# Delta by ScalarE's softplus, read from the side bank, in a macaron block of gated FFNs around a state-space layer

## The reference

```python
xn = x * rsqrt(mean(x * x) + EPS) * norm_w
skip = xn @ W_skip.T
u = silu(causal_conv4(xn @ W_in.T) + conv_b)
delta = softplus(u @ Wd1.T @ Wd2.T + bd2)            # 1024 x 512 for each batch
Bt, Ct, A = u @ WB.T, u @ WC.T, -exp(A_log)
h_l = exp(delta_l * A) * h_(l-1) + (delta_l * u_l) * B_l    # scan over 512 positions, 16 states
y_l = sum over states of h_l * C_l
out = ((y + u * W_D) * silu(skip)) @ W_out.T
```

## Time and profile before

| | |
|---|---|
| Median of 3 runs | 4050.57 us (4049.12 to 4053.82) |
| Profiled execution | 4051.71 us, its span 4050.0 us |
| Log blocks | 16, the first starting at 345.9 us, the last at 3558.7 us |
| Scan | the first Exp of a unit at 360.5 us, the last product with C starts at 3826.4 us |

### The profile page before, as it was taken

The page is one execution under the profiler, slowest core; times in us unless marked ns, Lnnn a source line. Parts: engine busy times, 40 slices in busy tenths (PEclk is TensorE's granted clock), DMA queues, the critical chain, the costliest instruction groups (busy, mean ns, idle before and its releaser), DMA issues. The chain is left out here.

```text
span 4050.0 us, 38161 instructions
## 1 busy us (share of the span) xinstructions
PE 3607.4 (89%) x11264; PEld 2077.2 (51%) x11264; DVE 3205.8 (79%) x3392; ACT 2039.0 (50%) x2694; POOL 2918.7 (72%) x2249
## 2 busy tenths in 40 slices
PE   7998889999999999899999898899887788787798
PEld 5654555555555555554555454545454344444455
DVE  4425988787989789887999889977988789989823
ACT  3234557547554664557554755466353665353310
POOL 0024789677977899688886998779967989878700
PEclk9999999999999999999999999999898898888899
DMA  6444545544645465354554555546454345444432
GB/s 234 148 134 140 162 147 168 201 148 148 211 159 182 146 202 191 120 187 154 201 172 154 173 164 188 155 139 202 156 171 133 124 148 180 148 126 148 122 123 90
DMA packets 233148, 647.64 MB, mean 160 GB/s; under 512 B 25968, under 2 KB 26224, under 8 KB 223216
## 3 DMA queue, kind: packets, MB, share of 16 engines
q1 hardware_dynamic: 159216, 510.95, 37.0%
q10 hardware_dynamic: 73728, 134.25, 12.5%
HBM read 579.57 MB, written 65.54 MB: 159 GB/s over the span
## 5 line engine op out<-in xcount | busy, mean ns | idle before, releaser
L1096 POOL TENSOR_TENSOR db<-du,Bb 128x512 f32<-128x512 f32 x1024 | 1357.5, 1326 | 539.8 <-DVE decay L990 459.9
L990 DVE TENSOR_TENSOR_SCAN decay<-decay,db 128x512 f32<-128x512 f32 x1024 | 1251.9, 1223 | 268.7 <-ACT decay L690 253.8
L1107 POOL TENSOR_TENSOR y<-y,pr 128x512 f32<-128x512 f32 x1024 | 1382.8, 1350 | 63.9 <-DVE pr L1000 63.9
L690 ACT ACTIVATE decay<-delta,aneg 128x512 f32<-128x512 f32 x1024 | 701.5, 691 | 1187.3 <-DVE pr L1000 1181.1
L523 PE MATMUL main<-zhi,wunit 128*128 128x512 f32 x2048 | 961.4, 469 | 54.4 <-DVE zlo L934 32.5
L582 PE MATMUL side<-h,wdown 128*128 128x512 f32 x2048 | 925.0, 595 | 16.1 <-DVE res_r L975 8.8
L524 PE MATMUL main<-zlo,wunit 128*128 128x512 f32 x2048 | 811.2, 396 | 0.0
L525 PE MATMUL main<-zhi,wunit 128*128 128x512 f32 x2048 | 809.8, 395 | 0.0
L1000 DVE TENSOR_TENSOR pr<-decay,Cb 128x512 f32<-128x512 f32 x1024 | 703.2, 687 | 31.5 <-DVE decay L990 0.3
L582 PEld LDWEIGHTS side<-h,wdown 128*128 128x128 f32 x2048 | 389.0, 190 | 425.6 <-issue 389.1
L598 PE MATMUL side<-xm,wmam 128*128 128x512 f32 x1024 | 488.4, 624 | 60.2 <-ACT cv L771 28.1
(11 more groups left out here) (80 smaller groups left out, 2624.2 us busy)
## 6 DMA issues: line engine op xcount, KB each, us to landing
wunit<-hl_dram SPq DMA_DIRECT2D x480, 512.0 KB, 3.8
wdown<-down_w_dram SPq DMA_DIRECT2D x256, 256.0 KB, 2.9
Bb<-bc_dram ACTq DMA_DIRECT2D x256, 256.0 KB, 3.9
Cb<-bc_dram ACTq DMA_DIRECT2D x256, 256.0 KB, 5.0
wmam<-mam_w_dram SPq DMA_DIRECT2D x64, 512.0 KB, 3.9
hl_dram<-wunit SPq DMA_DIRECT2D x32, 512.0 KB, 2.9
skip_dram<-skb SPq DMA_DIRECT2D x64, 256.0 KB, 4.1
delta<-skip_dram SPq DMA_DIRECT2D x16, 1024.0 KB, 6.6
```

What stands on the lines that cost most here:

```text
L690: nc.scalar.activation(decay[u % BANKS][:], delta[:, e, :], ACT.Exp, scale=aneg[:, e, n:n + 1]).then_inc(sem["decay_ready"], 1)
L990: nc.vector.tensor_tensor_scan(decay[u % BANKS][:], decay[u % BANKS][:], db[u % RING][:], 0.0, ALU.mult, ALU.add).then_inc(sem["state_read ...
L1096: nc.gpsimd.tensor_tensor(db[u % RING][:], du[:, e, :], Bb[m % ROWS][:], ALU.mult).then_inc(sem["input_ready"], 1)
L1107: nc.gpsimd.tensor_tensor(y[:, e, :], y[:, e, :], pr[u % RING][:], ALU.add).then_inc(sem["sum_ready"], 1)
```

## The change

Delta's softplus is done by ACT's own function Softplus as each side bank is read, with the bias, so that `delta` is final after line 798's instruction. `log_terms` and `end_delta` are gone, and with them the places `log` and `delta` of the plan and three semaphores; `first_terms` and `delta_times_u` move three ticks earlier for half 0 of batches 1 to 6, two for batch 7, one or two for batch 0, and three ticks for half 1. Who waited for `delta_ready` now waits for the four reads of the half's side banks (`wait_delta`).

```diff
-SLOW = {"dt": 6, "bc": 7, "dl": 8, "log": 10, "delta": 12, "first": 13, "du": 14}
-FAST = {"dt": 4, "bc": 4, "dl": 5, "log": 6, "delta": 7, "first": 8, "du": 9}
-AT_START = {"dt": 10, "bc": 10, "dl": 11, "log": 12, "delta": 13, "first": 14, "du": 14}
+SLOW = {"dt": 6, "bc": 7, "dl": 8, "first": 10, "du": 11}
+FAST = {"dt": 4, "bc": 4, "dl": 5, "first": 6, "du": 7}
+AT_START = {"dt": 10, "bc": 10, "dl": 11, "first": 12, "du": 13}
...
-            self.log_at[late + 2] = (b, 1)
-            self.delta_at[late + 4] = (b, 1)
-            self.first_at[late + 5] = (b, 1)
+            self.first_at[late + 2] = (b, 1)
-            self.du_at[late + 6] = (b, 1)
+            self.du_at[late + 3] = (b, 1)
...
-            return cost + 2.3 * (tick in self.delta_at) + 3 * (tick in self.du_at)
+            return cost + 3 * (tick in self.du_at)
...
+        def wait_delta(eng, b, half):
+
+            for e in range(HE * half, HE * half + HE):
+                wait_read(eng, ("dl", b, e))
...
-                    act.wait_ge(sem["delta_ready"], 2 * b + half + 1)
+                    wait_delta(act, b, half)
...
-                nc.scalar.activation(delta[:, e, :], bank_of(key)[:], ACT.Identity,
+                nc.scalar.activation(delta[:, e, :], bank_of(key)[:], ACT.Softplus,
                                      bias=small[:, C_BD + e:C_BD + e + 1]).then_inc(read_of(key), 1)
 
-            def log_terms(b, half):
-
-                soft = y[:, halves[half], :]
-                step = 2 * (2 * b + half)
-                for e in range(HE * half + HE - 2, HE * half + HE):
-                    wait_read(act, ("dl", b, e))
+            def first_terms(b, half):
                 if half == 0:
                     wait_job(act, ("bc", b))
                 elif b:
                     wait_job(act, ("out", b - 1, 1, KD - 1))
+                    act.wait_ge(sem["u_loaded_2"], 16 * b)
                 if b == 0:
                     act.wait_ge(sem["split_ready"], FFN)
-                nc.scalar.activation(soft, delta[:, halves[half], :], ACT.Abs).then_inc(sem["log_step"], 1)
-                act.wait_ge(sem["log_step"], step + 1)
-                nc.scalar.activation(soft, soft, ACT.Exp, scale=-1.0).then_inc(sem["log_step"], 1)
-                act.wait_ge(sem["log_step"], step + 2)
-                nc.scalar.activation(soft, soft, ACT.Ln, bias=1.0).then_inc(sem["log_ready"], 1)
-
-            def first_terms(b, half):
-                act.wait_ge(sem["delta_ready"], 2 * b + half + 1)
-                if half and b:
-                    act.wait_ge(sem["u_loaded_2"], 16 * b)
...
-            def end_delta(b, half):
-                dve.wait_ge(sem["log_ready"], 2 * b + half + 1)
-                es = halves[half]
-                nc.vector.scalar_tensor_tensor(delta[:, es, :], delta[:, es, :], 0.0, y[:, es, :],
-                                               ALU.max, ALU.add).then_inc(sem["delta_ready"], 1)
-
             def delta_times_u(b, half):
                 dve.wait_ge(sem["first_term_ready"], HE * (2 * b + half + 1))
-                dve.wait_ge(sem["delta_ready"], 2 * b + half + 1)
+                wait_delta(dve, b, half)
```

More of the change, by code:

```diff
@@ L117, in __init__ @@
         self.dl_at = {}
-        self.log_at, self.delta_at, self.first_at, self.du_at = {}, {}, {}, {}
+        self.first_at, self.du_at = {}, {}
         self.gate_at, self.out_at = {}, {}
@@ L133, in __init__ @@
             late = STARTS[b] + 8
-            self.log_at[origin + chain["log"]] = (b, 0)
-            self.log_at[late + 2] = (b, 1)
-            self.delta_at[origin + chain["delta"]] = (b, 0)
-            self.delta_at[late + 4] = (b, 1)
             self.first_at[origin + chain["first"]] = (b, 0)
-            self.first_at[late + 5] = (b, 1)
+            self.first_at[late + 2] = (b, 1)
             self.du_at[origin + chain["du"]] = (b, 0)
-            self.du_at[late + 6] = (b, 1)
+            self.du_at[late + 3] = (b, 1)
             assert origin + chain["du"] < STARTS[b], b
@@ L319, in build @@
             "decay_ready", "input_ready", "state_ready", "weighted_ready", "sum_ready",
-            "conv_step", "conv_ready", "u_ready", "delta_copied",
-            "log_step", "log_ready", "delta_ready", "first_term_ready", "du_ready", "gated_ready", "dve_step",
+            "conv_step", "conv_ready", "u_ready",
+            "first_term_ready", "du_ready", "gated_ready", "dve_step",
             "const_ready", "aneg_ready", "high_ready", "split_ready",
@@ L880, in _ @@
                         squares(key[1], 1)
-                if tick in plan.log_at:
-                    log_terms(*plan.log_at[tick])
                 if tick in plan.first_at:
@@ L1066, in _ @@
                     gate(*plan.gate_at[tick])
-                if tick in plan.delta_at:
-                    end_delta(*plan.delta_at[tick])
                 if tick in plan.du_at:
```

## The result

The changed kernel takes 3976.8 us (median of 4 runs, 3973.1 to 3977.6) against 4049.9 (4 runs): ratio 0.9818, 95% interval 0.9805 to 0.9831, so 73 us less. The forecast was 4016, 35 us less: the direction was right and 3977 lies in the range of 3972 to 4056, but the gain is over twice the one forecast, and 3977 lies near the edge of the forecast's own range of 3972 to 4037. The chip ran the profiled execution in 3973.1 us.

The account below looks back on a forecast made before the run. TensorE sets the time, idle 10.7% of the scan behind late VectorE comparisons. Gain 63 us less switch costs (10 + 9) x 1.47 = 28 gives 35 us, so 4016 us from a profiled 4051.7; range 3972 to 4056.

Parts of the forecast that it names:

- the forecast's own range: Whole kernel: the time range for the forecast as costed, a gain of 15 to 80 us, chance 0.62.
- The chain: At log blocks: ScalarE held 8.9 us, VectorE dry 5.96 us, comparison late, TensorE idle 8.45 us.
- the gain term of 63 us: TensorE's idle and slow-clock time after the 16 log blocks: middle of bounds 25 and 101 us.
- the moved steps: First terms and delta times u up to three ticks earlier: inputs amply covered, cost unchanged, put at nothing.
- the cost of the switches: Softplus table loads, 19 more than before: VectorE 10 and side banks 9, times 1.47, 28 us lost.
- VectorE's part, 10 us: In 29 scan groups 0.8 us reach VectorE, 23 us; TensorE feels it at the 45% late comparisons.
- The side banks' part of 9 us: Softplus' load delays the read that frees a bank by 1.28 us; between 4 and 38, taken as 9.
- The price of the clock: TensorE in the scan: 0.47 us lost to the lower clock for each idle us, 162 / 348.
- Given back (1): Rival: log-block waits go, but TensorE stands at the next late comparison; about 4054 us, chance 0.15.
- One table (2): Rival: Softplus and Exp share a table, 31 loads go and none comes; 3988 us, chance 0.06.
- Dearer switches (3): Rival: ScalarE's table switches cost more than the log block did; about 4104 us, slower, chance 0.11.
- What would show it: Signs: 30 Softplus groups, ScalarE near 1971 us, VectorE near 3161, fewer waits, TensorE's scan idle about 320.

Follow-up runs that it names:

- 8: Changed kernel with scan units in the ticks of before, first terms sooner, delta times u alone back at its old places: 3991.6 us.
- 9: Changed kernel with scan units in the ticks of before, first terms and delta times u sooner for the first halves alone: 3988.3 us.
- run 7: Kernel before with 14 of its 16 log blocks split in three pieces, scan units between them where the planner has any: 4030.3 us.
- 4: Changed kernel with first terms, delta times u and the planner's charges back at the places of the kernel before: 3994.0 us.
- 10: Changed kernel with scan units in the ticks of before, first terms and delta times u sooner for the second halves alone: 3980.7 us.
- 5: Changed kernel with steps at their new places but scan units in exactly the ticks of the kernel before: 3976.9 us.
- a version made after that theory: Changed kernel, units as before, first terms and delta times u at old places in first halves of batches 2 to 7, sooner elsewhere: 3976.7 us.
- 11: Changed kernel with four delta times u products moved one tick later, off a comparison's tick, the planner following: 3987.8 us.
- 12: Changed kernel with the same four delta times u products one tick later, but units in the changed kernel's ticks: 3978.1 us.

## Why the prediction was wrong

- **The chain** (block on ScalarE, dry VectorE, late comparison, idle TensorE) was right, and the gain term of 63 us was too: block and joining by themselves measure 37 + 25 = 62. It was got as the middle of two bounds that lay 76 us apart, so that it fits to 1 us is luck. It should have been made of its two parts, the 44.5 us on VectorE, which are worth 25, and the 92 us on ScalarE with 40 us of loads, which are worth 37.
- **The step that failed first** is that of the moved steps: "come up to three ticks earlier and cost what they did", costed at nothing. The places are worth 17 us (3994 against 3977). I had asked only whether their inputs would be there in time, not what else their place changes. The runs 8 and 9 show that it is delta times u that has to be early, not the first terms. Why is shown for one place alone, where the product lets POOL go just ahead of VectorE's wide work; it was in the trace of before for anyone who looked at VectorE's timeline there: comparisons and scaling in batch 1 took 5.62 and 6.79 us beside POOL's 2.71.
- **The second term that was mis-sized** is the cost of the switches: 28 us forecast (10 + 9, with the clock), 8 measured. I took the mean of 1.8 us that ScalarE stands before an Exp as the cover for 2.57 us and let the rest reach VectorE each time. The two decay banks give VectorE an Exp in hand as well; behind the first group of reads shown above it stood for 1.07 us, and behind the second for no Exp at all (its 3.05 us there are a wait for the first terms). The side banks' part of 9 us was not too large by the waits: those behind the reads grew from 8.4 us to 17.4, weight loads and matmuls counted together, and of the matmuls alone from 3.3 to 6.6. So it is VectorE's part, 10 us, that was too large, and how the 8 us divide isn't measured.
- 63 + 17 - 8 = 72, and 73 is measured. The two errors were 17 and 20 us and both made the forecast gain too small.
- **The price of the clock**, 0.47 us for each us of idle, was near: 0.40.
- **The rivals.** Given back (1) is wrong: the lead grows through the scan and is kept to the end. One table (2) is wrong by its count, 30 loads before the reads. Dearer switches (3) is wrong for the 50 loads of this change and right for the next 64: these 64 give 50 us back of 73. The Trainium skill's price of about 2.66 us a switch (ScalarE: Activation LUTs, What ACT_TABLE_LOAD costs) isn't seen: at 2451.57 a load starts, at 2452.86, 1.29 us later, the Exp behind it.
- **What would show it**: ScalarE's and VectorE's sums, the 30 groups, VectorE's waits for an Exp and TensorE's for comparisons went as forecast; TensorE's idle time in the scan fell to 296 us, further than the 320 forecast. The waits for comparisons are no measure of the gain, though: in run 7, with all its records, they are 147.0 us, 11 more than before, in a kernel that is 19 us faster.

Open: why the second halves' products being early is worth 13 us. In the traces it stands with VectorE's waits for an Exp: 242.7 and 242.9 us in the runs with them late (9 and 4), 227.0 and 229.7 with them early (10 and 5); what makes the Exps late isn't shown. The collision was shown for one place alone (11 to 12 us when it alone is late, but 4 us when all first halves are), a version made after that theory gave nothing, and the parts (6 for the first halves, 13 for the second) don't split as it says. Among changes of this kind 10 us can also come from the planner's placement by itself (runs 11 and 12).

## What to carry to other kernels

A moved step is not free because its inputs are ready and its own time stays the same. Ask whom it releases and what work stands there, and measure the places by themselves: here they were worth 17 us, and one instruction three ticks later cost 11 us where the engine it let go ran against wide work of its neighbour (though not when others were late as well). Extra time on an engine that is half idle costs little while waits and buffers cover it, and then about half of what it is: 62 us of table loads for 8, the next 91 for 50. So keep such switches in short holds that buffers cover, and don't merge them past the number of banks. Bounds from a share of idle time (25 to 101 us here) are too wide to forecast with: measure each part by taking it away by itself.

## What the runs showed of the hardware

VectorE and POOL hinder each other on tiles in SBUF, by far more than I had thought. A [128, 2048] product of two SBUF tiles on VectorE takes 2.28 us alone and took 7.28 with POOL running four instructions back to back, ending 2.14 us after the last of them; three comparisons took 5.62 instead of 3.50. The scan and the product with C, whose first operand is in PSUM, showed none of it: all 1024 scans took between 1.21 and 1.23 us and all 1024 products between 0.67 and 0.70. The Trainium skill (SBUF — State Buffer, SBUF: two separate sides) says that VectorE, in an operation with two SBUF inputs, and GpSimd share a pair of ports by an exclusive lock and that the loser blocks fully. The trace agrees with that page where VectorE's product ended about its own 2.28 us, 2.14 by the records, after POOL's last; that POOL's own instructions also lasted 1.7 to 2.7 us instead of 1.27 would fit two engines that take the lock in turn, which no run here shows by itself.

Softplus from a PSUM bank with a bias takes what Identity takes (684 and 680 ns), and stands behind a table load of 1.283 us of its own, 30 for 30 groups between other functions.
